# Mixture of experts: half the tokens sorted by expert into 23 blocks of 128 rows, between dense units of the other half

## The reference

```python
shared_out = (silu(xf @ sw1) * (xf @ sw3)) @ sw2          # 128 -> 256 -> 128
logits = xf @ router_w.T + experts_bias                   # 8 experts
rw, sel = top_k(logits, 2); rw = softmax(rw)
cw = (one_hot(sel, 8) * rw[..., None]).sum(axis=1)        # weight of each expert, 6 of 8 are 0
g = einsum('td,edh->teh', xf, w1); u = einsum('td,edh->teh', xf, w3)
moe_out = einsum('te,teh,ehd->td', cw, silu(g) * u, w2)
return moe_out + shared_out
```

## Time and profile before

| | |
|---|---|
| median of 3 runs | 1084.19 us (1081.42 to 1084.34) |
| the profiled execution, its own time | 1078.49 us |
| its span, first to last instruction | 1076.8 us |
| mean granted TensorE clock | 0.925 of full speed |
| busy: PE, DVE, ACT, POOL | 933.8, 708.1, 619.6, 337.8 us |
| ffn0 call 0, first to last gate instruction | about 24 to 183 us of the span |
| ffn0 call 1 | about 494 to 653 us |

### The profile page before, as it was taken

The page is one execution under the profiler, slowest core; times in us unless marked ns, Lnnn a source line. Parts: engine busy times, 40 slices in busy tenths (PEclk is TensorE's granted clock), DMA queues, the critical chain, the costliest instruction groups (busy, mean ns, idle before and its releaser), DMA issues.

```text
span 1076.8 us, 13026 instructions
## 1 busy us (share of the span) xinstructions
PE 933.8 (87%) x4507; PEld 628.2 (58%) x4507; DVE 708.1 (66%) x1413; ACT 619.6 (58%) x1003; POOL 337.8 (31%) x249
## 2 busy tenths in 40 slices
PE   6899999579999999879999997799967777777997
PEld 4678887123333333337788876488644545455886
DVE  3978887467778777646788886744276556547532
ACT  6555555268888888863555555544554545455454
POOL 1597777000000000001677775201201221123200
PEclk8999999689999999997999998699988778888999
DMA  5125110000000000003311110200000000001001
GB/s 172 43 79 159 66 62 27 0 1 0 1 1 1 0 1 0 1 0 118 76 64 64 64 50 16 63 21 2 1 0 3 4 2 2 4 1 39 1 2 40
DMA packets 30743, 33.64 MB, mean 31 GB/s; under 512 B 2062, under 2 KB 19798, under 8 KB 30678
## 3 DMA queue, kind: packets, MB, share of 16 engines
q1 hardware_dynamic: 30678, 32.81, 9.9%
HBM read 31.36 MB, written 1.18 MB: 30 GB/s over the span
## 4 chain that ended last, share of the span: by engine, by line
PE 61%; DVE 19%; ACT 11%; issue 4%; POOL 3%; DMA 0%; ACTq 0%; SPq 0%; DVEq 0%; POOLq 0%
PE ps L128 10%; PE ps L129 10%; PE ps L130 10%; PE ps L750 5%; PE ps L862 4%; PE ps L744 2%; ACT ex L1485 2%; PE ps L955 2%; PE ps L728 2%; ACT L1374 2%; POOL fl L2155 2%; DVE smax L2034 1%; PE ps L891 1%; PE ps L964 1%; PE ps L736 1%
## 5 line engine op out<-in xcount | busy, mean ns | idle before, releaser
L2155 POOL TENSOR_TENSOR fl<-fp,fh 128x512 fp32r<-128x512 f32 x144 | 223.5, 1568 | 126.3 <-ACT fh L1280 126.0
L1271 ACT ACTIVATE fs<-ps 128x512 f32<-128x512 f32 x144 | 86.2, 599 | 114.6 <-PE ps L130 114.4
L1743 DVE TENSOR_TENSOR fp<-fp,cwb 128x512 f32<-128x512 f32 x128 | 141.2, 1103 | 14.0 <-DVE fp L1736 0.9
L1736 DVE TENSOR_TENSOR fp<-fs,ps 128x512 f32<-128x512 f32 x144 | 98.2, 682 | 40.7 <-ACT fs L1271 40.1
L128 PE MATMUL ps<-z_hi,w_hi 128*128 128x512 f32 x288 | 117.0, 406 | 3.3 <-DVE fp L1736 3.3
L129 PE MATMUL ps<-z_lo,w_hi 128*128 128x512 f32 x288 | 116.6, 405 | 0.0
L130 PE MATMUL ps<-z_hi,w_lo 128*128 128x512 f32 x288 | 115.0, 399 | 0.0
L1280 ACT CAST fh<-fp 128x512 fp32r<-128x512 f32 x144 | 88.8, 617 | 36.8 <-DVE fp L1743 32.6
L2219 POOL TENSOR_TENSOR ln_sq<-ln_rs 128x512 f32<-128x512 f32 x20 | 21.1, 1056 | 272.4 <-ACT ln_rs L1337 272.4
L2212 POOL TENSOR_SCALAR_AFFINE_SELECT ex<-ex 128x1024 f32<-128x1024 f32 (+1 forms) x24 | 33.4, 1403 | 152.4 <-ACT ex L1485 152.4
L2034 DVE TENSOR_REDUCE smax<-ps 128x8 f32<-128x2048 f32 (+1 forms) x24 | 55.0, 2291 | 38.8 <-PE ps L969 31.9
(11 more groups left out here) (270 smaller groups left out, 2005.2 us busy)
## 6 DMA issues: line engine op xcount, KB each, us to landing
cwb<-cw_spread SPq DMA_DIRECT2D x64, 256.0 KB, 3.1
w_raw<-in_L_ffn_w_dram SPq DMA_DIRECT2D x20, 256.0 KB, 2.9
w_raw<-in_L_ffn_w_dram SPq DMA_DIRECT2D x4, 512.0 KB, 5.9
w<-in_L_ffn_w_dram SPq DMA_DIRECT2D x8, 256.0 KB, 4.4
x_tok<-in_L_attn_x_dram SPq DMA_DIRECT2D x4, 256.0 KB, 3.5
wb<-in_L_attn_W_dram SPq DMA_DIRECT2D x1, 1024.0 KB, 7.0
wb<-in_L_attn_W_dram SPq DMA_DIRECT2D x4, 256.0 KB, 4.0
out_dram<-z SPq DMA_DIRECT2D x4, 256.0 KB, 3.0
```

Source lines behind the costliest of these rows:

```text
L1271: act.activation(fs[:, n % 2, :], ps[:, n % 2, :], ACT.Silu).then_inc(silu_done, 1)
L1736: dve.tensor_tensor(f, fs[:, n % 2, :], ps[:, 2 + n % 2, :], ALU.mult).then_inc(prod_done, 1)
L1743: dve.tensor_tensor(f, f, cwb[:, x % CW_RING, :], ALU.mult).then_inc(weighed, 1)
L2155: pool.tensor_tensor(fl[:, n % RING0, :], fp[:, n % RING0, :], f32(fh[:, n % RING0, :]), ALU.subtract).then_inc(flo_done, 1)
```

## The change

Blocks 0 and 1 of the tokens stay dense: 8 shared units for all four blocks and 16 units for each of the two, `ALL0 = 40`. Blocks 2 and 3 (1024 tokens, two experts each, 2048 rows) are sorted by expert. Each expert's rows are filled up to a multiple of 128; with 8 experts that is at most 23 blocks (`BLOCKS0 = 2 * ST + EXP - 1`, `ST = 8` token tiles), and 23 are always run. The steps:

- **Row store.** `tokens_turned` transposes `z_hi` and `z_lo` of the 8 token tiles on TensorE (16 transposes), `tokens_copied` brings them to `zt` on ScalarE, `store_rows` on SP writes `z_dram`, 1 KB a token.
- **Routing.** `ranks()` counts with 9 small bf16 products how many earlier tokens chose each expert. `ranked`, `slots`, `slot_parts`, `block_hot`, `row_hot` on VectorE turn that into each row's block and place, spread over units 8 to 17. `table()` (16 bf16 products, at unit 19) inverts it, and `rows` and `owners` give for each block the token rows to `take`, the rows to `give` to, and the expert (`owner`).
- **Blocks.** For block b: `gather(b)` on GpSimd is an indirect DMA of 128 rows from `z_dram` to `xg`; `rows_in(b)` transposes both halves on TensorE (bank `x_bank`), ScalarE copies them to `xs`; `rows_up(b)` reads the expert from `owner` into a register and does three products of 512 columns (gate and up side by side in one bank, `gu_bank`); `rows_gate` on ScalarE, `rows_product` on VectorE; `hidden_turned(b)` transposes the 256 hidden columns back (bank `t_bank`), `hidden_high` on ScalarE and `hidden_low` on VectorE split them; `rows_down(b)` does four products of 256 columns; `rows_out` on VectorE adds the two halves into `ys`, and `scatter(b)` on GpSimd is an indirect DMA to `y_dram`.
- **Order.** The 16 dense units of block 1 are mixed with sorted blocks 0 to 15 (`MIXED0`), blocks 16 to 22 follow (`LATE0`). In the mixed part `low(n)` stands on VectorE and no longer on GpSimd.
- **Sum.** `load_sums` on SP waits for all scatters and loads both results of each token (four loads of 256 KB), `weigh_rows` on VectorE multiplies them, `summed` on TensorE transposes and adds them, `add_summed` puts them on `xr`. The shared expert's part of blocks 2 and 3 is added by `add_shared` during units 14 and 15.
- **Call 1's end.** The `LN_FFN1` steps follow the last sorted block; the top rounds stand behind `weigh_rows` and after the first of them the `add_summed`.

The expert weights are kept as one tile `w0` with high and low parts next to each other in pieces of 128 columns, so that one product can read both (`rows_down`). `load_blocks` starts at the eighth spread weight.

The core of the diff, TensorE:

```diff
-                for n in range(1, ALL0):
+                for n in range(1, PLAIN0):
                     up(n)
                     if n >= LAG0:
                         down(n - LAG0)
+                    if n in (1, 2):
+                        tokens_turned(2 * n - 2)
+                        tokens_turned(2 * n - 1)
                     if n == LAG0 + 1:
                         weights()
+                    if n == LAG0 + 2:
+                        ranks()
+                    if n == PLAIN0 - 5:
+                        table()
+                owners = {}
+                rows_in(0)
+                for b in range(MIXED0):
+                    n = PLAIN0 + b
+                    rows_in(b + 1)
+                    owners[b] = rows_up(b)
+                    if b >= 1:
+                        rows_down(b - 1, owners[b - 1])
+                    up(n)
+                    hidden_turned(b)
+                    down(n - LAG0)
+                for b in LATE0:
+                    owners[b] = rows_up(b)
+                    if b + 1 < BLOCKS0:
+                        rows_in(b + 1)
+                    if b == MIXED0:
+                        rows_down(b - 1, owners[b - 1])
+                    elif b > MIXED0 + 1:
+                        rows_down(b - 2, owners[b - 2])
+                    if b - MIXED0 < LAG0:
+                        down(ALL0 - LAG0 + b - MIXED0)
+                    if b > MIXED0:
+                        hidden_turned(b - 1)
+                hidden_turned(BLOCKS0 - 1)
+                for b in range(BLOCKS0 - 2, BLOCKS0):
+                    rows_down(b, owners[b])
```

TensorE's new functions, with their waits:

```diff
+                def rows_in(b):
+                    pe.wait_ge(xg_in[b % XG_RING], 16 * gathered_in(call, b))
+                    if b == 0:
+                        pe.wait_ge(route_vector, TV(call, "owners"))
+                    elif b == 1:
+                        pe.wait_ge(rows_scalar, RS(call, "in", 0))
+                    elif b <= MIXED0:
+                        pe.wait_ge(rows_vector, RV(call, "low", b - 2))
...
+                    for half in range(2):
+                        ins = pe.transpose(ps[:, x_bank(b), half * P:(half + 1) * P], xg[:, b % XG_RING, half * P:(half + 1) * P], ident[:])
+                def rows_up(b):
+                    pe.wait_ge(rows_scalar, RS(call, "in", b))
...
+                    e = pe.value_load(owner[0:1, b:b + 1], min_val=1, max_val=EXP)
+                    hi, lo = (w0[:, bass.ds(e, 1), 0:2 * HT0, half, :].rearrange("p a c n -> p (a c) n") for half in range(2))
+                    out = ps[:, gu_bank(b), :]
+                    x_hi, x_lo = xs[:, b % 2, 0:P], xs[:, b % 2, P:2 * P]
+                    pe.matmul(out, x_hi, hi, start=True, stop=False)
+                    pe.matmul(out, x_hi, lo, start=False, stop=False)
+                    pe.matmul(out, x_lo, hi, start=False, stop=True).then_inc(rows_matmul, 1)
+                def rows_down(b, e):
+                    pe.wait_ge(rows_vector, RV(call, "low", b))
...
+                    for t in range(HT0):
+                        w = w0[:, bass.ds(e, 1), 2 * HT0 + t, :, :].rearrange("p a h n -> p (a h n)")
+                        h = slice(t * P, (t + 1) * P)
+                        pe.matmul(out, sh_hi[:, b % 2, h], w, start=(t == 0), stop=False)
+                        ins = pe.matmul(out, sh_lo[:, b % 2, h], w, start=False, stop=(t == HT0 - 1))
```

VectorE in the mixed part, and at the end of both calls; ScalarE's order there is `rows_in(b + 1)`, `rows_gate(b)`, `high(n - 1)`, `gate(n)`, `hidden_high(b)`:

```diff
+                for b in range(MIXED0):
+                    n = PLAIN0 + b
+                    if b >= 1:
+                        rows_out(b - 1)
+                    rows_product(b)
+                    low(n - 1)
+                    product(n)
+                    hidden_low(b)
+                    weigh(n)
...
+                if call == 0:
+                    for tb in range(NTB - DENSE0):
+                        weigh_rows(tb)
+                    for tb in range(NTB - DENSE0):
+                        add_summed(tb)
+                else:
                     dve.wait_ge(sc_ready, part1(0, 0) + 1)
                     ln_root(LN_FFN1, 0, SPB - 1)
                     part_weights(0, LN_FFN1, 0)
+                    for tb in range(NTB - DENSE0):
+                        weigh_rows(tb)
                     chances(0, 0)
                     top_start(0, 0)
-                    top_rounds(0, 0, range(CAP // 8))
+                    top_rounds(0, 0, range(1))
+                    for tb in range(NTB - DENSE0):
+                        add_summed(tb)
+                    top_rounds(0, 0, range(1, CAP // 8))
                     top_end(0, 0)
```

GpSimd, behind its low halves of units 0 to 21 (`LOW0`):

```diff
+                pool.wait_ge(zt_stored, 16 * (ST // 2) * (call + 1))
+                pool.wait_ge(route_vector, TV(call, "rows"))
+                for b in range(XG_RING):
+                    gather(b)
+                for b in range(BLOCKS0):
+                    if b + XG_RING < BLOCKS0:
+                        gather(b + XG_RING)
+                    scatter(b)
```

More of the change, by code:

```diff
@@ L93, with steps0, mark, matmul_order0 @@
 WB = 4 * P + 2 * F1
+def steps0(order):
+    def mark(call, name, b=0):
+        return call * len(order) + order.index((name, b)) + 1
+    return mark
+LATE0 = range(MIXED0, BLOCKS0)
+def matmul_order0():
+    order = [("in", 0)]
+    for b in range(MIXED0):
+        order += [("in", b + 1), ("up", b), ("down", b - 1), ("turn", b)]
+    for b in LATE0:
+        order += [("up", b), ("in", b + 1), ("down", b - 1 if b == MIXED0 else b - 2), ("turn", b - 1)]
+    order += [("turn", BLOCKS0 - 1), ("down", BLOCKS0 - 2), ("down", BLOCKS0 - 1)]
+    return once(order)
+def scalar_order0():
+    order = [("in", 0)]
+    for b in range(MIXED0):
+        order += [("in", b + 1), ("gate", b), ("high", b)]
+    for b in LATE0:
+        order += [("gate", b), ("in", b + 1), ("high", b - 1)]
+    return once(order + [("high", BLOCKS0 - 1)])
+def vector_order0():
+    order = []
+    for b in range(MIXED0):
+        order += [("out", b - 1), ("product", b), ("low", b)]
+    for b in LATE0:
+        order += [("product", b), ("out", b - 1 if b == MIXED0 else b - 2), ("low", b - 1)]
+    return once(order + [("low", BLOCKS0 - 1), ("out", BLOCKS0 - 2), ("out", BLOCKS0 - 1)])
+def once(order):
+    return list(dict.fromkeys(x for x in order if 0 <= x[1] < BLOCKS0))
+RM, RS, RV = steps0(matmul_order0()), steps0(scalar_order0()), steps0(vector_order0())
+TM = steps0([("tokens", n) for n in range(ST // 2)] + [("rank", 0), ("table", 0)])
+TV = steps0([("chosen", 0), ("place", 0), ("hot", 0), ("rows", 0), ("owners", 0)])
 def a0_roles(period):
@@ new lines, in rows @@
+                def rows():
+                    dve.wait_ge(route_matmul, TM(call, "table"))
+                    a_, b_, v_ = (ps[:, IDX_BANK, k * BLOCKS0:(k + 1) * BLOCKS0] for k in range(3))
+                    own.did(dve.scalar_tensor_tensor(out=unused[:], in0=v_, scalar=-1.0, in1=spare[:], op0=ALU.add, op1=ALU.mult))
+                    own.wait()
+                    own.did(dve.scalar_tensor_tensor(out=dest_f[:], in0=b_, scalar=float(P), in1=unused[:], op0=ALU.mult, op1=ALU.subtract))
+                    own.wait()
+                    own.did(dve.tensor_tensor(give[:], dest_f[:], a_, ALU.add))
+                    own.wait()
+                    dve.tensor_scalar(take[:], give[:], SROWS - 1, None, ALU.bitwise_and).then_inc(route_vector, 1)
@@ L1773, in ffn0 @@
                 choose()
-                for n in range(4, ALL0):
+                for n in range(4, PLAIN0):
                     product(n)
```

449 lines of the change are left out of this document (386 added, 63 removed).

## The result

The changed kernel takes 1155.28 us, median of 4 runs (1148.81 to 1158.36). The kernel before took 1084.26 us beside it (4 runs, 1081.42 to 1089.11). The ratio is 1.0642, with a 95% interval of 1.0581 to 1.0704: slower by 6.4%, where 1139 us (5.1%) had been forecast. Its profiled execution took 1158.36 us with a span of 1155.0, against a span of 1076.8: 78.2 us to explain. The medians lie 71.0 us apart. The profiled execution of the changed kernel is the slowest of its four and that of before (1078.49) a fast one, so some 7 of the 78.2 us are what one execution differs from another.

The account below looks back on a forecast made before the run. TensorE was taken as full in each call's later part. Calls 7.0 + 2.6, routing 11.1, ranks 4.0, transposes 4.0, first gathers 7.4, reads 18.4 add 54.5 us: 1133.0 profiled, 1139 as median, range 1085 to 1180.

Parts of the forecast that it names:

- The mixed steps: Sixteen steps a call of dense unit plus sorted block: bank 6 loop of 5.0 us each, 80.0, reads extra.
- The owner read: Register read before each block's up products: 0.85 us, 0.4 open, 46 times, 18.4 us in all.
- What a sorted block costs TensorE: Transposes and products of one 128-row block: 2.06 us, like a dense unit; 10.5 us a call to gain.
- the first rival: Other engines' steps hide behind TensorE, only its issue time counts: 21 us saved, 1063 us; chance 0.12.
- The late steps: Seven sorted blocks without dense up: four at 2.76, three at 2.06, TensorE bound, 17.2 us a call.
- Routing: VectorE's added work in units 8 to 23: 11.7 us a call, 5.2 and 5.9 left after filling idle time.
- Up to unit 8: Token transposes on TensorE: 3.5 us a call, partly in a gap, 2.0 taken, 4.0 in all (0 to 7).
- The first gather: Start of the mixed part: TensorE waits 3.7 us a call for gathered rows, 7.4 in all (0 to 10).
- The drains: After the last sorted block, scatter, reload, weighing, sums: 17.0 us for 6.9 in call 0, 30.2 for 24.5 in call 1.
- Reads and routing hidden: Rival: the register read is covered and routing fits VectorE's idle time, 1109 us; chance 0.17.
- The dear read: Rival: a register read costs 1.5 us, giving 1171 us, or 3.1, giving 1245; chance 0.12.
- GpSimd as the bound: Rival: building one gather and one scatter at 3.1 us each makes mixed steps 6.2, 1169 us; chance 0.08.

Follow-up runs that it names:

- run 1: Changed kernel with gathered rows of blocks 9 to 16 transposed into PSUM bank 4 instead of shared bank 6: 1130.5 us, ratio 1.0424.
- run 2: Changed kernel with a constant expert per sorted block in place of the register read, so results are not those asked for: 1128.23 us, ratio 1.0379.
- run 4: Changed kernel with ScalarE's high half ahead of the dense gate and VectorE's low half ahead of the dense product: 1136.6 us, ratio 1.049.
- Run 8: Changed kernel with bank 4 from block 6, run 4's order, owner read one product ahead, call 1's tail reordered: 1108.8 us, ratio 1.0246.
- run 12: Run 8 plus earlier first gather, reload awaited in two pairs, and call 1's weight loads behind the first four spread loads: 1100.88 us, ratio 1.0172.
- run 5: Changed kernel with VectorE making the ranks' one-hot row chunks twice, 32 more instructions: 1162.63 us, ratio 1.0736.
- run 7: Changed kernel with each owner read placed one product ahead, results as asked: 1135.35 us, ratio 1.0479.
- run 3: Changed kernel with both edits, own bank for rows of blocks 9 to 16 and a constant expert instead of the read: 1114.43 us, ratio 1.0267.

## Why the prediction was right, and where its sizes were off

The direction and the mechanism held, and the mixed steps, the largest part, were right within 2%, in part because two slips cancel (below). As a median 1138.7 was forecast and 1155.28 measured, 16.6 us more. Against the sum as profiled (1133.0), the profiled span is 23.7 us longer than 1076.8 + 54.5. By its steps:

- **The mixed steps** were given a loop of 5.0 and 0.4 for the read, 5.4; the trace shows 5.54. Sixteen steps took 87.65 us from the first up to the seventeenth, against 86.4. Runs 1, 2 and 4 each removed one part of the loop that the prediction had put into it: the shared bank 1.58 us (its own wait, and the read that could then be covered), the read 0.64, the two instructions queued ahead 0.60.
- **The owner read** was given 0.4 open; it was 0.46 idle in the record and 0.64 in the step (run 2). That it is covered once nothing stands before it (run 1) was not foreseen. The Trainium skill, DMA: Bandwidth & Descriptors (Latency and other measured facts), gives a tensor load a floor near 0.6 us; the 0.64 of run 2 is near it, though it is what the step pays and no row shows the read's own time.
- **What a sorted block costs TensorE** was misread. The eight records of the earlier trace rows are eight transposes of one pass, not four of two: the changed kernel's L866 has 92 records for 46 blocks of two transposes. A transpose costs 0.109, a sorted block 1.62 instead of 2.06, and a mixed step has a floor of 0.22 + 0.70 + 0.48 + 1.39 + 0.22 + 0.70 = 3.71 instead of 4.15. Run 8's 3.78 shows it. The gain on offer was 22.4 us a call, not 10.5. The slip hardly moved the forecast, by luck: the transposes in stand in the loop and ahead of the read, so with 0.22 in place of 0.44 the loop is 4.78 and not 5.0 (run 2, without the read, shows 4.90), and 0.63 of the assumed 0.85 us stays open and not 0.4 (0.64 was measured). The two changes cancel. It also made the first rival look poorer than it was.
- **The late steps** were given 17.2 and 2.8 for reads, 20.0. They took 19.45, from 189.62 to 209.07. That they were TensorE bound does not hold: with transposes at one pass, TensorE's part is 14.1 us. In the trace of call 0 it stood idle there six times for 0.4 to 1.0 us, 4.1 us in all: for ScalarE three times, for VectorE, for a gather and for "issue". No experiment was made on these. Without reads (run 2) the late stretch is 1.9 and 1.8 us shorter.
- **Routing** was given 5.2 and 5.9, and 2.0 a call for ranks and table on TensorE. Units 8 to 23 took 44.7 us against 35.8 in call 0 and 42.9 against 31.4 in call 1: 8.9 and 11.5. VectorE's added work in call 0 was 13.0 us for the 11.7 given, and 2.3 us of its idle time stayed unfilled. The one-hot chunks were priced at 0.25 and average 0.41, two thirds more. In call 1 there is the wait for spread weights too, 3.5 us behind 12 weight loads on SP, which the prediction had set to nothing. Its 42.9 us are near the upper end of what traces of the same code show (40.2 to 43.1).
- **Up to unit 8** it was given 2.0 a call for the token transposes; 5.0 and 2.0 came. In call 0 the logits ran at half clock there. That isn't shown to be the change's: the gate of unit 8 of call 0 stands at 50.88, and at 47.6 to 51.3 in the traces of the runs, whose code is the same up to there.
- **The first gather**: 3.7 was given, 3.39 and 3.71 idle were measured. But the sum had nothing for the way from the first transposes in to the first up, with both a copy and a read in the open: 2.35 us a call. From the gate of unit 23 to that first up it takes 6.4 and 6.7 us, 5.7 more than the two 3.7.
- **The drains** were the largest miss, 17.0 and 30.2 against 20.6 and 34.1. The load took 6.2 for the 5.8 given and the scatter 2.3 for the 3.1. Weighing, second sum and add took 8.7 (220.90 to 229.64) for the 5.3 given. The sums had been counted at full clock: 32 passes took 6.57 and 6.67 us, 0.21 a pass, at a granted clock of 0.50 nearly throughout. In call 0 TensorE had stood idle for 11 us, in call 1 for 2.8 us.
- **Behind the stages** unchanged code took 3.7 us more, with a lower granted clock in one window (0.74 against 0.82). The prediction said only that the clock was not priced. Executions of one kernel differ by as much.
- **The stretch of before** was counted as 100.3 us in both calls. From the gate of unit 23 to that of unit 71 it is 100.5 us in call 0 and 102.2 in call 1.
- **The signs.** The spacing of the gates, the low-half wait, the "issue" idle and the gap at the first gather came as written. The "15 us and more without TensorE work" at the end of call 0 were 11.0, and the top rounds of call 1 did not start behind a DMA wait.

The differences are 3.0 up to unit 8, 5.3 for routing, 5.7 for the start of the mixed steps, 1.3 for steps and late steps, 7.5 for drains and 3.7 behind, less 0.6 between the calls and 2.1 for the stretch of before: 23.8, the 23.7 but for rounding.

Of the rivals, TensorE's issue time alone (1063) never came: even run 12 stays at 1100.88. "Reads and routing hidden" (1109) is right for the reads if the order is changed and wrong for the routing (run 5, call 0 above all). The dear read falls with run 2. GpSimd as the bound falls with its own row, which shows it waiting 129.5 us for VectorE's output:

```profile
L2653 POOL DMA_INDIRECT y_rows<-ys,give x46 | 45.3, 984 | 129.5 <-DVE ys L2143 129.5
```

Open are what holds the late steps, and what the token transposes and the ranks cost apart from VectorE's work.

## What to carry to other kernels

Replacing dense work with sorted work moves the bound from TensorE's work to chains: sum one step's loop through shared banks and queue orders, with the result latency, before counting products. An unqueued engine pays twice, once for the wait and once for everything whose latency queued work had covered, so one buffer can be worth more than the wait that it removes (run 1: 1.58 us a step for a wait of 0.93). Price what is added where another engine is nearly full already (here VectorE in units 8 to 23) at its full work, and price drains at the lower clock, which the sums of both drains had here.

## What the runs showed of the hardware

- A register read from SBUF ahead of a matmul whose address depends on it costs 0.64 us a step where TensorE has just waited for its input (5.54 against 4.90). It costs 0.13 with a turn, a dense down and two transposes in between (run 7, 5.03 against 4.90) and under 0.1 where TensorE's queue is full (run 1 against run 3).
- An indirect transfer of 128 rows keeps GpSimd for 0.97 us as a gather and 0.98 as a scatter (medians). The median from issue to landing is 2.8 us for a gather and 2.3 for a scatter. The Trainium skill, DMA: Bandwidth & Descriptors (Anatomy of one DMA), gives GpSimd-built transfers a fixed cost near 2.0 us; the medians, which hold the moving of the bytes too, are 0.3 to 0.8 more. The gathers' row, of the view of one line:

```profile
DMA to landing us min/median/max: 2.7/2.8/8.1
```

- A 128x128 transpose has one record and takes 0.109 us at full clock (92 records for the 92 transposes in). The sums, of the same shape against the same identity, have two records per product (32 for 16 in each call).
- After 11 us without work TensorE took 6.57 us for 32 passes that would be 3.5 at 0.109 each. All but the last microsecond ran at the lower of its clocks, 1.2 GHz, a granted clock of 0.50. The windows of call 0, then of call 1, where TensorE had been idle for 2.8 us only:

```profile
222.00:228.00 6.00, 5.75 (x27) 5.75 (x28) 2.09 (x4) 0.00 (x0) 0.00 (x0) 0.50 0.01 3
228.00:229.00 1.00, 0.81 (x7) 0.62 (x6) 0.15 (x1) 0.00 (x0) 0.00 (x0) 1.00 0.00 0
```

```profile
730.60:736.00 5.40, 5.37 (x25) 5.37 (x26) 2.39 (x6) 2.38 (x7) 2.67 (x2) 0.50 0.01 3
```
